# Cross-attention, one core: inputs transposed on the host, high parts converted by DMAs from GpSimd's queue

## The chip, the cores and the metric

The kernel runs on one NeuronCore of a Trainium2 chip. The metric is the device time of one execution in microseconds; the times shown are of three executions.

## The reference

`x` is (64, 256, 512), `ctx` is (64, 256, 384), all float32; the weights are (512, 512), (384, 512) and (512, 512).

```
Q = layer_norm(x @ W_text + b_text) * g1 + beta1
V = ctx @ W_audio + b_audio
K = layer_norm(V) * g2 + beta2
alpha = softmax(Q @ K.T / sqrt(512))          # per batch, 256 x 256
y = layer_norm((alpha @ V) @ W_out + b_out + x) * g_out + beta_out
```

## The kernel before, in words

The 64 batches are worked in N = 32 steps of two batches (512 tokens, T = 4 tiles of 128 rows). Every float32 matmul is made of three fp32r matmuls: each operand is split into a rounded high part and the rest, the low part, and hi\*hi + lo\*hi + hi\*lo are summed in PSUM (`product`, L253 to L255). Means are folded into the weights at the start; `W_audio` and `W_out` are multiplied together once (`wao`).

A step i does this, with j = i - 1, whose second half is worked off between:

- TensorE transposes ctx (`turn_c`, 3 groups of 4 transposes, for step i + 1) and x (`turn_x`, 4 groups) into the PSUM banks `turn`; ScalarE casts each bank to the high part (`cT_high`, `xT_high`), VectorE subtracts that from the bank to get the low part (`cT_low`, `xT_low`, the helper `low`, L613).
- `project_k`, `project_q` multiply them by the weights; ScalarE centres and squares. The sum of squares is made of `pair_squares` on GpSimd (L866), `add_square` (L637) and `sum_squares` (L645) on VectorE, `turn_sum` on TensorE and `sum_rows` on VectorE; GpSimd makes the reciprocal root (`row_rstd`, L872 and L874), and TensorE spreads it (`spread_rs`). VectorE scales (`k_norm`, `q_norm`) and makes low parts.
- `scores`, the softmax, and one step later `turn_p`, `probs_context` (context rows `c_hi`, `c_lo`, which GpSimd splits in `split_c`) and `output`.
- The residual: GpSimd adds the bias row to x into `y_rows[odd]` (`bias_x`, L895). VectorE adds the product (`y_sum`) and takes statistics, GpSimd makes scales (`y_scale`, L857 to L861), ScalarE normalises, GpSimd finishes (`finish_y`, L901, L903), SP stores (`store_y`).

There are two buffers `y_rows`, for even and odd steps. `y_rows[odd]` of step i is that of step i - 2, whose tiles 2 and 3 are finished and stored within step i.

There is no scheduler. Each engine has its queue in the order in which its block of the program is written, and waits on semaphores. The two orders that matter here:

- GpSimd's step: pair the squares of k, `finish_y(i-2)` for tiles 2 and 3, `row_rstd` of k, `bias_x` 0 and 1, pair the squares of q, `bias_x` 2 and 3, `row_rstd` of q, `split_c`, then the scales and `finish_y` of j for tiles 0 and 1. The first `bias_x` waits for all four tiles of x.
- SP's step: store tiles 2 and 3 of i - 2, copy `c_in` to `c_kept`, load `c_in` for i + 1, load the four tiles `x_in` for i + 1 (each when `bias_x` of step i has read it), store tiles 0 and 1 of i - 1.

`run_steps` writes steps 0, 1, N-2 and N-1 out and loops over pairs of the others.

Of the kernel before, what the change touches and what calls it, by code (L numbers as in the profile page):

```python
# [10 lines left out]
ALU = mybir.AluOpType  # L11
# [3 lines left out]
P = 128  # L15
# [3 lines left out]
def cross_attention_kernel(nc, x, ctx, w_text, b_text, w_audio, b_audio, w_out, b_out,  # L19
                           g1, beta1, g2, beta2, g_out, beta_out, out):  # L20

    B, L, D = x.shape
    S, DC = ctx.shape[1], ctx.shape[2]
    H = w_text.shape[1]
    NB = 2
    N = B // NB
    DT, CT, HT = D // P, DC // P, H // P  # L40
    LT, ST = L // P, S // P
    T = NB * LT
# [3 lines left out]
    x_v = x.rearrange("(i b) (t p) d -> i p (b t) d", b=NB, p=P)  # L46
    c_v = ctx.rearrange("(i b) (t p) d -> i p (b t) d", b=NB, p=P)
    out_v = out.rearrange("(i b) (t p) d -> i p (b t) d", b=NB, p=P)

    with ExitStack() as stack:  # L50
# [27 lines left out]
        x_in, c_in = sb("x_in", [P, T, D]), sb("c_in", [P, T, DC])  # L78
# [38 lines left out]
        x_loaded, c_loaded, c_copied = sem("x_loaded"), sem("c_loaded"), sem("c_copied")  # L117
# [15 lines left out]
        xT_done, cT_done = sem("xT_done"), sem("cT_done")  # L133
# [4 lines left out]
        xT_hi_made, cT_hi_made = sem("xT_hi_made"), sem("cT_hi_made")  # L138
# [49 lines left out]
        def _(sp):  # L188
            def load_c(i):
                sp.dma_start(c_in[:], c_v[i]).then_inc(c_loaded, 16)  # L190

            def load_x(i, t):
                sp.dma_start(x_in[:, t, :], x_v[i, :, t, :]).then_inc(x_loaded, 16)

            sp.dma_start(wa_stage[:, 0:CT, :], w_audio.rearrange("(t p) h -> p t h", p=P)).then_inc(wa_loaded, 16)
            load_c(0)
# [7 lines left out]
            for t in range(T):  # L204
                load_x(0, t)
# [4 lines left out]
            def store_y(j, odd, t):  # L210
                wait_apart(sp, y_ready, T * j + t + 1)
                sp.dma_start(out_v[j, :, t, :], y_rows[odd][:, t, :]).then_inc(stored[t], 16)

            def step(i, odd, first=False, last=False):
# [5 lines left out]
                wait_apart(sp, c_loaded, 16 * (i + 1))  # L220
                sp.dma_start(c_kept[:], c_in[:]).then_inc(c_copied, 16)
                if not last:
                    wait_apart(sp, c_copied, 16 * (i + 1))
                    wait_apart(sp, cT_done, CT * (i + 1))
                    load_c(i + 1)
                    wait_apart(sp, xT_done, DT * (i + 1))
                    for t in range(T):
                        wait_apart(sp, x_biased, T * i + t + 1)
                        load_x(i + 1, t)
# [15 lines left out]
        def _(pe):  # L245
# [32 lines left out]

            def turn_x(i, d):
                if d == 0:  # L280
                    pe.wait_ge(x_loaded, 16 * T * (i + 1))
                transposes(turn[d % 2], [x_in[:, t, d * P:(d + 1) * P] for t in range(T)]).then_inc(xT_done, 1)

            def turn_c(i, d):
                to = score[1] if d == 2 and isinstance(i, int) and i == 0 else turn[d % 2]
                if d == 0:
                    pe.wait_ge(c_loaded, 16 * (i + 1))
                transposes(to, [c_in[:, t, d * P:(d + 1) * P] for t in range(T)]).then_inc(cT_done, 1)
# [79 lines left out]
            for d in range(CT):  # L368
                turn_c(0, d)
# [5 lines left out]
            def step(i, odd, first=False, last=False):  # L375
# [53 lines left out]
                if not last:  # L429
                    pe.wait_ge(k_normed, HT * (i + 1))  # L430
                    turn_c(i + 1, 0)
                    pe.wait_ge(q_normed, HT * (i + 1))
                    turn_c(i + 1, 1)
                pe.wait_ge(kT_split, HT * (i + 1))
                scores(i, 0, 0)
                if not last:
                    pe.wait_ge(cT_split, CT * (i + 1) + 1)
                    turn_c(i + 1, 2)
# [22 lines left out]
        def _(act):  # L461
            def xT_high(i, d):
                act.wait_ge(xT_done, DT * i + d + 1)
                wait(act, q_done, T * i)
                nc.scalar.copy(xT_hi[:, d, :], turn[d % 2][:]).then_inc(xT_hi_made, 1)

            def cT_high(i, d):
                act.wait_ge(cT_done, CT * i + d + 1)
                wait(act, k_done, T * i)
                of = score[1] if d == 2 and isinstance(i, int) and i == 0 else turn[d % 2]  # L470
                nc.scalar.copy(cT_hi[:, d, :], of[:]).then_inc(cT_hi_made, 1)

# [70 lines left out]
            for d in range(CT):  # L543
                cT_high(0, d)
# [439 lines left out]
```

## Time and profile before

| | |
|---|---|
| time, median of 3 | 1487.2 us (1487.1, 1487.2, 1487.49) |
| span of the profiled execution | 1486.0 us |
| TensorE busy, share of the span | 1436.8 us, 97% |
| VectorE | 1147.9 us, 77% |
| GpSimd | 1050.5 us, 71% |
| ScalarE | 855.9 us, 58% |
| TensorE's granted clock, mean | 0.998 of full speed |
| HBM read, written | 62.40 MB, 33.55 MB |

The span reaches from the first to the last instruction. A time of the profiled execution itself is not listed beside its span; the three executions' times lie 1.1 to 1.5 us above it. Busy is the time in which at least one instruction of the engine runs; matmuls overlap each other, so their mean duration is longer than their pitch.

### The profile page before, as it was taken

Reading aid. Unit: us, or ns where it says so; the run is one execution under the profiler, and the core shown is the slowest. Engines: PE = TensorE matmul, PEld = TensorE weight load, DVE = VectorE, ACT = ScalarE, POOL = GpSimd, SP = SyncE. Lnnn points to the kernel's source line nnn. Section 1 sums busy time; section 2 is a strip of 40 time slices with the busy share of each in tenths; the row PEclk is TensorE's granted clock in tenths of the full one; section 3 lists DMA queues with packets and bytes.
Section 4 is the critical chain, followed back from the end, with each engine's and each line's share of the span. In section 5 each row is a group of like instructions: output and inputs, shape, how many; then the busy total and the mean of one; then the engine's idle time right before and its main releaser. Section 6 shows DMA issues by size and latency. Waiting matters only on the chain.

```text
span 1486.0 us, 26150 instructions
## 1 busy us (share of the span) xinstructions
PE 1436.8 (97%) x8240; PEld 1219.4 (82%) x8240; DVE 1147.9 (77%) x1657; ACT 855.9 (58%) x1547; POOL 1050.5 (71%) x1223
## 2 busy tenths in 40 slices
PE   8999999999999999999999999999999999999996
PEld 6788888888888888888888888888888888888885
DVE  6578777887777887777887778877778877788777
ACT  5465666555665555665556656556655466655563
POOL 2466777667867667776678676677776777766786
PEclk9999999999999999999999999999999999999999
DMA  5212221122221122211222211222212222112211
GB/s 191 71 43 86 100 99 53 67 85 92 99 99 46 66 90 93 99 67 53 85 92 99 99 49 64 92 92 99 84 43 78 92 99 99 51 67 87 93 50 58
DMA packets 63449, 121.44 MB, mean 82 GB/s; under 512 B 8385, under 2 KB 24769, under 8 KB 63425
## 3 DMA queue, kind: packets, MB, share of 16 engines
q1 hardware_dynamic: 63424, 121.14, 22.6%
q8 instruction: 12, 0.20, 0.1%
q14 instruction: 13, 0.10, 0.0%
HBM read 62.40 MB, written 33.55 MB: 65 GB/s over the span
## 4 chain that ended last, share of the span: by engine, by line
PE 33%; DVE 28%; POOL 23%; issue 12%; ACT 2%; DVEq 1%; SPq 1%; POOLq 0%; DMA 0%; ACTq 0%
POOL y_rows L901 8%; DVE qT_lo L663 8%; POOL y_rows L903 5%; DVE y_rows L685 5%; PE wide L255 5%; PE wide L253 5%; PE wide L254 5%; DVE q_cols L657 4%; PE turn L260 4%; DVE y_bn L690 3%; DVE row_max L700 3%; POOL squares L866 2%; DVE cT_lo L613 2%; POOL y_sc L859 2%; PE score L253 2%
## 5 line engine op out<-in xcount | busy, mean ns | idle before, releaser
L253 PE MATMUL wide<-xT_hi,wt_hi 128*128 128x512 f32 x512 | 209.9, 410 | 0.0
L255 PE MATMUL wide<-xT_hi,wt_lo 128*128 128x512 f32 x512 | 202.0, 395 | 0.0
L254 PE MATMUL wide<-xT_lo,wt_hi 128*128 128x512 f32 x512 | 201.9, 394 | 0.0
L895 POOL TENSOR_TENSOR y_rows<-x_in,bao_row 128x512 f32<-128x512 f32 x128 | 176.6, 1401 | 9.5 <-DVE bao_row L738 9.5
L507 ACT ACTIVATE qT_hi<-q_cols,beta_col 128x512 fp32r<-128x512 f32 x128 | 90.6, 725 | 154.7 <-DVE q_cols L657 154.7
L903 POOL TENSOR_TENSOR y_rows<-y_rows,betao_row 128x512 f32<-128x512 f32 x124 | 170.2, 1372 | 9.7
L901 POOL TENSOR_TENSOR y_rows<-y_rows,go_row 128x512 f32<-128x512 f32 x124 | 173.8, 1402 | 0.0
L657 DVE SCALAR_TENSOR_TENSOR k_cols<-k_cols,g_col,turn 128x512 f32<-128x512 f32 x128 | 89.6, 740 | 100.3 <-PE turn L260 100.3
L487 ACT ACTIVATE squares<-wide,btc_col 128x512 f32<-128x512 f32 x128 | 88.2, 689 | 135.4 <-PE wide L255 134.1
L857 POOL TENSOR_SCALAR y_sc<-y_mv 128x1 f32<-128x1 f32 x128 | 24.4, 191 | 192.6 <-DVE y_mv L695 187.2
L253 PE MATMUL wide<-cT_hi,wa_hi 128*128 128x512 f32 x384 | 159.3, 415 | 0.0
L335 PE MATMUL wide<-wao_hi,pcT_hi 128*128 128x512 f32 x384 | 154.2, 402 | 0.0
L255 PE MATMUL wide<-cT_hi,wa_lo 128*128 128x512 f32 x384 | 151.8, 395 | 0.0
L337 PE MATMUL wide<-wao_hi,pcT_lo 128*128 128x512 f32 x384 | 151.8, 395 | 0.0
L336 PE MATMUL wide<-wao_lo,pcT_hi 128*128 128x512 f32 x384 | 151.7, 395 | 0.0
L253 PE MATMUL score<-kT_hi,qT_hi 128*128 128x256 f32 x512 | 150.0, 293 | 1.4 <-DVE qT_lo L663 1.4
L254 PE MATMUL wide<-cT_lo,wa_hi 128*128 128x512 f32 x384 | 151.1, 393 | 0.0
L255 PE MATMUL score<-kT_hi,qT_lo 128*128 128x256 f32 x512 | 144.6, 282 | 0.0
L254 PE MATMUL score<-kT_lo,qT_hi 128*128 128x256 f32 x512 | 144.6, 282 | 0.0
L512 ACT ACTIVATE y_rows<-y_rows,y_sc 128x512 f32<-128x512 f32 x128 | 106.0, 828 | 62.7 <-POOL y_sc L861 62.7
L663 DVE SCALAR_TENSOR_TENSOR qT_lo<-q_cols,beta_col,qT_hi 128x512 fp32r<-128x512 f32 x128 | 138.0, 1096 | 4.4
L887 POOL TENSOR_TENSOR c_lo<-c_kept,c_hi 128x384 fp32r<-128x384 f32 x128 | 129.9, 1015 | 10.7
(116 smaller groups left out, 4081.1 us busy)
## 6 DMA issues: line engine op xcount, KB each, us to landing
x_in<-in_x SPq DMA_DIRECT2D x128, 256.0 KB, 4.3
out<-y_rows SPq DMA_DIRECT2D x128, 256.0 KB, 2.0
c_in<-in_ctx SPq DMA_DIRECT2D x32, 768.0 KB, 4.6
c_kept<-c_in SPq DMA_DIRECT2D x32, 768.0 KB, 3.5
q_cols<-in_L_xattn_W_text SPq DMA_DIRECT2D x1, 1024.0 KB, 5.6
y_rows<-in_L_xattn_W_out SPq DMA_DIRECT2D x1, 1024.0 KB, 8.1
k_cols<-in_L_xattn_W_audio SPq DMA_DIRECT2D x1, 768.0 KB, 4.7
bao_row<-in_L_xattn_b_out SPq DMA_DIRECT2D x1, 256.0 KB, 8.3
```

The lines of the kernel that those rows point to most:

```text
L253: nc.tensor.matmul(to, a_hi, b_hi, start=(m == 0), stop=False)
L254: nc.tensor.matmul(to, a_hi, b_lo, start=False, stop=False)
L255: done = nc.tensor.matmul(to, a_lo, b_hi, start=False, stop=(m == n - 1))
L335: nc.tensor.matmul(wide[t][:], hi, wao_hi[:, d, :], start=(d == 0), stop=False)
L336: nc.tensor.matmul(wide[t][:], hi, wao_lo[:, d, :], start=False, stop=False)
L337: done = nc.tensor.matmul(wide[t][:], lo, wao_hi[:, d, :], start=False, stop=(d == CT - 1))
L657: nc.vector.scalar_tensor_tensor(out=cols[:, h, :], in0=cols[:, h, :], scalar=gain[:, h:h + 1], in1=rs[:], op0=ALU.mult, op1=ALU.mult).the ...
L663: nc.vector.scalar_tensor_tensor(out=lo[:, h, :], in0=cols[:, h, :], scalar=shift[:, h:h + 1], in1=hi[:, h, :].bitcast(F32), op0=ALU.add, ...
L887: nc.gpsimd.tensor_tensor(c_lo[:, t, :], c_kept[:, t, :], c_hi[:, t, :].bitcast(F32), ALU.subtract).then_inc(c_split, 1)
L895: nc.gpsimd.tensor_tensor(y_rows[odd][:, t, :], x_in[:, t, :], bao_row[:], ALU.add).then_inc(x_biased, 1)
L901: nc.gpsimd.tensor_tensor(rows, rows, go_row[:], ALU.mult).then_inc(y_scaled, 1)
L903: nc.gpsimd.tensor_tensor(rows, rows, betao_row[:], ALU.add).then_inc(y_ready, 1)
```

## The change

The host lays out four arrays in place of two: `x_rows` and `c_rows` (per step, partition and tile, so that a partition's data is contiguous) and `xT` and `cT` (the transposes that TensorE made before). The output is written in the layout of `x_rows` and put back on the host.

- TensorE: `turn_x` and `turn_c` are gone.
- ScalarE: `xT_high` and `cT_high` are gone. GpSimd issues one DMA for each that reads `xT[i]` or `cT[i]` from HBM and converts it to fp32r on its way to `xT_hi` or `cT_hi`.
- VectorE: `xT_low` and `cT_low` subtract that from `xT_in` and `cT_in`, which SP loads from the same arrays; both inputs are in SBUF now.
- The rows of x are loaded by SP straight into `y_rows[odd]`, and `bias_x` adds the bias in place. The rows of ctx are loaded straight into `c_kept`. The tiles `x_in` and `c_in` are gone.

```diff
             def step(i, odd, first=False, last=False):
...
-                wait_apart(sp, c_loaded, 16 * (i + 1))
-                sp.dma_start(c_kept[:], c_in[:]).then_inc(c_copied, 16)
+                load_c(i)
                 if not last:
-                    wait_apart(sp, c_copied, 16 * (i + 1))
-                    wait_apart(sp, cT_done, CT * (i + 1))
-                    load_c(i + 1)
-                    wait_apart(sp, xT_done, DT * (i + 1))
-                    for t in range(T):
-                        wait_apart(sp, x_biased, T * i + t + 1)
-                        load_x(i + 1, t)
+                    wait_apart(sp, cT_split, CT * (i + 1))
+                    load_cT(i + 1)
...
+                for t in range(T):
+                    if not isinstance(i, int) or i >= 2:
+                        wait_apart(sp, stored[t], 16 * (i - 1))
+                    load_x(i, odd, t)
+                if not first and not last:
+                    wait_apart(sp, xT_split, DT * (i + 1))
+                    load_xT(i + 1)
...
             def xT_low(i, d):
-                dve.wait_ge(xT_hi_made, DT * i + d + 1)
-                low(xT_lo[:, d, :], turn[d % 2][:], xT_hi[:, d, :]).then_inc(xT_split, 1)
+                dve.wait_ge(xT_loaded, 16 * (i + 1))
+                dve.wait_ge(xT_hi_loaded, 16 * (i + 1))
+                low(xT_lo[:, d, :], xT_in[:, d, :], xT_hi[:, d, :]).then_inc(xT_split, 1)
...
+            def load_xT_high(i):
+                if not isinstance(i, int) or i > 0:
+                    wait_apart(pool, q_done, T * i)
+                nc.gpsimd.dma_start(xT_hi[:], xT[i]).then_inc(xT_hi_loaded, 16)
+
+            def load_cT_high(i):
+                if not isinstance(i, int) or i > 0:
+                    wait_apart(pool, k_done, T * i)
+                nc.gpsimd.dma_start(cT_hi[:], cT[i]).then_inc(cT_hi_loaded, 16)
...
                 if t == 0:
                     pool.wait_ge(x_loaded, 16 * T * (i + 1))
-                wait(pool, stored[t], 16 * (i - 1))
-                nc.gpsimd.tensor_tensor(y_rows[odd][:, t, :], x_in[:, t, :], bao_row[:], ALU.add).then_inc(x_biased, 1)
+                rows = y_rows[odd][:, t, :]
+                nc.gpsimd.tensor_tensor(rows, rows, bao_row[:], ALU.add).then_inc(x_biased, 1)
...
                 row_rstd(i, k_ssq_made, k_ssq, k_ve, k_rs, k_var, k_rstd)
+                if not last:
+                    load_cT_high(i + 1)
...
+                if not last:
+                    load_xT_high(i + 1)
                 for t in range(T):
                     split_c(i, t)
```

SP's queue before, a step of the loop, from the store of tile 3 of step i - 2 (`out` is the store; the bracket says which semaphore is waited for):

```order
L212 DMA out<-y_rows 128x512
L171 REGISTER_ALU
L171 ISA [waits c_split]
L221 DMA c_kept<-c_in 128x1536 [waits c_loaded]
L171 REGISTER_ALU [waits c_copied]
L190 ISA [waits cT_done]
L190 DMA c_in<-in_ctx 128x4x384
L171 REGISTER_ALU
L171 REGISTER_ALU [waits xT_done]
L193 ISA [waits x_biased]
L193 DMA x_in<-in_x 128x512
L171 REGISTER_ALU
```

and SP's queue in the changed kernel from the same store. The rows of x, which were for the next step, are now for this one and wait for the stores of step i - 2; a load of `cT_in` stands in front of them:

```order
L198 DMA out<-y_rows 128x512
L152 REGISTER_ALU
L177 ISA [waits c_split]
L177 DMA c_kept<-in_c_rows 128x1536
L152 ISA
L171 ISA [waits cT_split]
L171 DMA cT_in<-in_cT 128x1536
L152 ISA
L180 ISA [waits stored0]
L180 DMA y_rows<-in_x_rows 128x512
L180 ISA [waits stored1]
L180 DMA y_rows<-in_x_rows 128x512
```

The same pair of rows follows for tiles 2 and 3. The copy of c became a load, and the loads of x wait on `stored` in place of `x_biased`.

GpSimd's queue before, from the last `finish_y` of step i - 2:

```order
L903 TENSOR_TENSOR y_rows<-y_rows,betao_row 128x512 [waits y_scaled]
L171 REGISTER_ALU
L872 TENSOR_SCALAR k_ve<-k_ssq 128x4 [waits k_ssq_made]
L874 TENSOR_TENSOR k_rs<-k_ve,neg_half 128x4 [waits k_var]
L893 REGISTER_ALU
L165 ISA [waits x_loaded]
L895 TENSOR_TENSOR y_rows<-x_in,bao_row 128x512 [waits stored0]
L895 TENSOR_TENSOR y_rows<-x_in,bao_row 128x512 [waits stored1]
L866 TENSOR_TENSOR squares<-squares 128x512 [waits q_squared]
L895 TENSOR_TENSOR y_rows<-x_in,bao_row 128x512 [waits stored2]
L895 TENSOR_TENSOR y_rows<-x_in,bao_row 128x512 [waits stored3]
L872 TENSOR_SCALAR q_ve<-q_ssq 128x4 [waits q_ssq_made]
```

and in the changed kernel:

```order
L858 TENSOR_TENSOR y_rows<-y_rows,betao_row 128x512 [waits y_scaled]
L152 REGISTER_ALU
L827 TENSOR_SCALAR k_ve<-k_ssq 128x4 [waits k_ssq_made]
L829 TENSOR_TENSOR k_rs<-k_ve,neg_half 128x4 [waits k_var]
L152 REGISTER_ALU
L817 ISA [waits k_done]
L817 DMA cT_hi<-in_cT 128x1536
L848 REGISTER_ALU
L850 TENSOR_TENSOR y_rows<-y_rows,bao_row 128x512 [waits x_loaded]
L850 TENSOR_TENSOR y_rows<-y_rows,bao_row 128x512
L821 TENSOR_TENSOR squares<-squares 128x512 [waits q_squared]
L850 TENSOR_TENSOR y_rows<-y_rows,bao_row 128x512 x2
```

A DMA for `cT_hi` has come in behind k_rs; one for `xT_hi` comes behind q_rs, a few rows further on; the wait for x stands where it stood, and the waits for `stored` moved to SP's queue.

## Rows read from the trace of the kernel before

**Rows 1.** The page: engines' busy time, and the chain that ended last, by engine.

```profile
PE 1436.8 (97%) x8240; PEld 1219.4 (82%) x8240; DVE 1147.9 (77%) x1657; ACT 855.9 (58%) x1547; POOL 1050.5 (71%) x1223
...
PE 33%; DVE 28%; POOL 23%; issue 12%; ACT 2%; DVEq 1%; SPq 1%; POOLq 0%; DMA 0%; ACTq 0%
```

**Rows 2.** Timeline of POOL (start us, length, line, what, idle before), one step.

```profile
685.84 0.19 POOL L857 TENSOR_SCALAR y_sc<-y_mv 128x1 f32<-128x1 f32 x1 [4.60 <-DVE y_mv L695]
...
725.45 1.02 POOL L887 TENSOR_TENSOR c_lo<-c_kept,c_hi 128x384 fp32r<-128x384 f32 x1
731.07 0.19 POOL L857 TENSOR_SCALAR y_sc<-y_mv 128x1 f32<-128x1 f32 x1 [4.60 <-DVE y_mv L695]
```

**Rows 3.** Windows, one step: length, busy us of each engine, clock, DMA share, GB/s.

```profile
700.00:745.20 45.20, 44.29 (x258) 37.74 (x257) 35.43 (x52) 26.48 (x49) 32.99 (x39) 1.00 0.22 81
```

**Rows 4.** Timeline of POOL, around the end of the finish of step i-2.

```profile
700.86 1.63 POOL L903 TENSOR_TENSOR y_rows<-y_rows,betao_row 128x512 f32<-128x512 f32 x1
...
704.26 1.29 POOL L903 TENSOR_TENSOR y_rows<-y_rows,betao_row 128x512 f32<-128x512 f32 x1
...
706.90 2.53 POOL L895 TENSOR_TENSOR y_rows<-x_in,bao_row 128x512 f32<-128x512 f32 x2
709.38 1.75 POOL L866 TENSOR_TENSOR squares<-squares 128x512 f32<-128x512 f32 x1
```

**Rows 5.** Timeline of DVE, from the pairing of q's squares.

```profile
712.87 1.78 DVE L637 TENSOR_TENSOR squares<-squares 128x512 f32<-128x512 f32 x1
...
715.24 0.68 DVE L645 TENSOR_TENSOR square_sum<-squares 128x512 f32<-128x512 f32 x1
...
720.63 0.75 DVE L657 SCALAR_TENSOR_TENSOR q_cols<-q_cols,g_col,turn 128x512 f32<-128x512 f32 x1 [1.23 <-PE turn L260]
```

**Rows 6.** Timeline of PE: a group of transposes, and the two spreads.

```profile
699.78 0.60 PE L260 MATMUL turn<-ident,x_in 128*128 128x128 f32 x4
700.13 0.48 PE L253 MATMUL wide<-xT_hi,wt_hi 128*128 128x512 f32 x1
700.45 0.39 PE L254 MATMUL wide<-xT_lo,wt_hi 128*128 128x512 f32 x1
700.68 0.39 PE L255 MATMUL wide<-xT_hi,wt_lo 128*128 128x512 f32 x1
...
706.98 0.65 PE L260 MATMUL turn<-ident,k_rs 128*128 128x128 f32 x4 [0.45 <-POOL k_rs L874]
...
720.00 0.60 PE L260 MATMUL turn<-ident,q_rs 128*128 128x128 f32 x4
```

**Rows 7.** Groups by line: turns of c (busy, mean ns, idle before).

```profile
L260 PE MATMUL turn<-ident,c_in 128*128 128x128 f32 x380 | 54.3, 280 | 14.2 <-DVE cT_lo L613 14.2
```

**Rows 8.** Lines L613 and L637: ns min/median/max, first and last start.

```profile
L613 DVE TENSOR_TENSOR xT_lo<-turn,xT_hi x128: 675/681/692, 17.5 to 1425.1; 128x512 fp32r<-128x512 f32 x128
...
L637 DVE TENSOR_TENSOR squares<-squares x64: 675/1291/1786, 23.4 to 1436.7; 128x512 f32<-128x512 f32 x64
```

**Rows 9.** Timeline of SP's queue, one step (start us, length of issue).

```profile
706.38 0.50 SPq L221 DMA_DIRECT2D c_kept<-c_in  x1
710.28 0.41 SPq L190 DMA_DIRECT2D c_in<-in_ctx  x1
711.17 3.51 SPq L193 DMA_DIRECT2D x_in<-in_x  x4
```

**Rows 10.** The page: DMA issues (KB each, us to landing).

```profile
out<-y_rows SPq DMA_DIRECT2D x128, 256.0 KB, 2.0
```

**Rows 11.** Tile x_in, 690 to 750 us: landing.

```profile
DMA to landing us min/median/max: 3.3/4.4/4.5
```

**Rows 12.** Windows of 1 us: DMA share and GB/s in the last two columns.

```profile
711.00:712.00 1.00, 1.00 (x6) 0.83 (x5) 1.00 (x2) 1.00 (x3) 1.00 (x2) 1.00 0.45 61
...
714.00:715.00 1.00, 1.00 (x11) 1.00 (x10) 1.00 (x2) 0.92 (x3) 0.10 (x1) 1.00 1.07 408
...
716.00:717.00 1.00, 1.00 (x10) 1.00 (x10) 1.00 (x2) 0.59 (x1) 0.00 (x0) 1.00 0.92 305
```

More of the change, by code:

```diff
@@ L76, in cross_attention_kernel @@
         g2_col, beta2_col = sb("g2_col", [P, HT]), sb("beta2_col", [P, HT])
-        x_in, c_in = sb("x_in", [P, T, D]), sb("c_in", [P, T, DC])
+        xT_in, cT_in = sb("xT_in", [P, DT, T * P]), sb("cT_in", [P, CT, T * P])
         c_kept = sb("c_kept", [P, T, DC])
@@ L188, in _, with load_cT, load_xT, load_x @@
         def _(sp):
+            def load_cT(i):
+                sp.dma_start(cT_in[:], cT[i]).then_inc(cT_loaded, 16)
+            def load_xT(i):
+                sp.dma_start(xT_in[:], xT[i]).then_inc(xT_loaded, 16)
             def load_c(i):
-                sp.dma_start(c_in[:], c_v[i]).then_inc(c_loaded, 16)
-            def load_x(i, t):
-                sp.dma_start(x_in[:, t, :], x_v[i, :, t, :]).then_inc(x_loaded, 16)
+                sp.dma_start(c_kept[:], c_rows[i]).then_inc(c_loaded, 16)
+            def load_x(i, odd, t):
+                sp.dma_start(y_rows[odd][:, t, :], x_rows[i, :, t, :]).then_inc(x_loaded, 16)
             sp.dma_start(wa_stage[:, 0:CT, :], w_audio.rearrange("(t p) h -> p t h", p=P)).then_inc(wa_loaded, 16)
-            load_c(0)
+            load_cT(0)
             columns = [(ba_col, b_audio), (bt_col, b_text), (g1_col, g1), (beta1_col, beta1),
@@ L211, in store_y @@
                 wait_apart(sp, y_ready, T * j + t + 1)
-                sp.dma_start(out_v[j, :, t, :], y_rows[odd][:, t, :]).then_inc(stored[t], 16)
+                sp.dma_start(out[j, :, t, :], y_rows[odd][:, t, :]).then_inc(stored[t], 16)
             def step(i, odd, first=False, last=False):
@@ L238, in _ @@
                 sp.wait_ge(last_ready[by], count)
-                sp.dma_start(out_v[N - 1, :, t, :], y_rows[1][:, t, :]).then_inc(stored[t], 16)
+                sp.dma_start(out[N - 1, :, t, :], y_rows[1][:, t, :]).then_inc(stored[t], 16)
             for t in range(T):
@@ L277, in project_q @@
                 product(wide[h][:], terms, xT_split if h == 0 else None, DT * i).then_inc(q_done, 1)
[L279 to L288, printed above, removed]
             def turn_sum(i, to, summed, turned):
@@ L396, in step @@
                 project_q(i, 0)
+                if not first:
+                    pe.wait_ge(pT_split, NB * j + 1)
                 turn_sum(i, turn[0], k_summed, k_sum_turned)
@@ L461, in _ @@
         def _(act):
[L462 to L471, printed above, removed]
             def pT_high(j, b):
@@ L542, in _ @@
             wa_high()
-            for d in range(CT):
-                cT_high(0, d)
             waT_copy(2)
@@ L615, in xT_low @@
             def xT_low(i, d):
-                dve.wait_ge(xT_hi_made, DT * i + d + 1)
-                low(xT_lo[:, d, :], turn[d % 2][:], xT_hi[:, d, :]).then_inc(xT_split, 1)
+                dve.wait_ge(xT_loaded, 16 * (i + 1))
+                dve.wait_ge(xT_hi_loaded, 16 * (i + 1))
+                low(xT_lo[:, d, :], xT_in[:, d, :], xT_hi[:, d, :]).then_inc(xT_split, 1)
             def cT_low(i, d):
-                dve.wait_ge(cT_hi_made, CT * i + d + 1)
-                of = score[1] if d == 2 and isinstance(i, int) and i == 0 else turn[d % 2]
-                low(cT_lo[:, d, :], of[:], cT_hi[:, d, :]).then_inc(cT_split, 1)
+                dve.wait_ge(cT_loaded, 16 * (i + 1))
+                dve.wait_ge(cT_hi_loaded, 16 * (i + 1))
+                low(cT_lo[:, d, :], cT_in[:, d, :], cT_hi[:, d, :]).then_inc(cT_split, 1)
             def pT_low(j, b):
```

82 lines of the change are left out of this document (35 added, 47 removed).

## The prediction, made before the change was run

> **What bounds the kernel now.** I read the page first. TensorE is busy 97% of the span and the others 58 to 77% [rows 1], which invites the reading that TensorE is the bound and that each transpose taken away is won. The chain of the last work says otherwise: TensorE has 33% of it, VectorE 28%, GpSimd 23% [rows 1]. So I went on to one step in the middle. All steady steps are alike: GpSimd's first small operation on y_sc starts at 685.84 and again at 731.07, 45.2 us apart [rows 2], and a stretch of 45.2 us shows TensorE busy 44.3, VectorE 35.4, ScalarE 26.5, GpSimd 33.0 at full granted clock, 2.4 GHz [rows 3].
>
> The loop that closes on itself is this. GpSimd ends the last finish_y of step i-2 at 704.26 + 1.29 = 705.55 (I call this moment A), makes k_rs, starts to bias x at 706.90, biases two tiles of x, pairs the squares of q until 711.1 [rows 4]. VectorE takes the paired squares at 712.87 and has square_sum at 715.92 [rows 5]. TensorE turns it, runs on, and spreads q_rs at 720.00 [rows 6]. VectorE starts q_norm at 720.63 [rows 5]. GpSimd's y_scale begins 10.44 us later, at 731.07, and from the same place of the step before (685.84) to A it takes 19.71 us [rows 2, 4]. 10.44 + 19.71 = 30.15 us of the 45.2 lie there. TensorE waits in it for k_rs, 0.45 us [rows 6], so it is filled nearly to the brim but does not close the loop alone.
>
> **What goes.** TensorE loses seven groups of four transposes a step. A group starts 0.35 us before the next matmul, whose own pitch is 0.32 instead of 0.23 [rows 6]: 0.44 us a group, 3.1 us a step; the wait before the third turn of c, 0.46 us a step (14.2 in the kernel), goes too [rows 7]. TensorE would then need 44.3 - 3.1 = 41.2 us. ScalarE loses seven casts; with 58% busy [rows 1] it was never the bound, and I count nothing for it. On SP the copy c_kept<-c_in goes.
>
> **What VectorE gets.** The seven subtractions stay, but both inputs lie now in SBUF, where before one was in PSUM. All 128 of xT_lo took 675 to 692 ns, whatever GpSimd did; the sum of squares, with two SBUF inputs, took 675 to 1786 ns [rows 8]. So the seven cost between 0 and 7 x 1.1 = 7.7 us of VectorE's time a step. Most start where VectorE has idle time; in the loop above they can hold GpSimd's two last finish_y pairs and VectorE's statistics. On GpSimd's side one such operation took 1.63 us and the next of its kind 1.29 [rows 4]. I take 0 for the sum, and 2 us a step as the upper end. The Trainium skill, SBUF — State Buffer, section "Who interferes with whom", says that a VectorE instruction with two SBUF inputs contends with a GpSimd instruction that reads SBUF and that the pair of ports is a lock; the two spreads agree with it. By that rule the sum would lie above my 0, toward the upper end.
>
> **What SP and GpSimd get, and here I see the end being set.** Before, x_in was loaded a step ahead (four issues at 711.17 to 714.68 for the next step), and bias_x found it there. Now the rows of x go straight into y_rows[odd], which hold the output of step i-2 until it is stored. SP's order is: store tiles 2 and 3 of step i-2, load c_kept, load cT_in, then the four tiles of x. The store of tile 3 waits for A; before, SP issued the next DMA behind it, the copy of c, at 706.38 [rows 9]. So nothing of this step's x is even issued before A. Behind it stand 786 KB of c, 786 KB of cT and 1,049 KB of x: 2.62 MB. (Tile 3 also waits for its own store, 2.0 us [rows 10], which passes under the issues in front of it.) GpSimd's first bias_x waits for all four tiles, and it stands in GpSimd's queue ahead of the pairing of q's squares.
>
> How late are they? The load of c_in issued at 710.28 shows its first bytes in the slice from 711, about 1.3 us on; then the DMA engines are full (share 1.05 to 1.07) at 395 to 408 GB/s; the last bytes come in the slice that ends at 717, while the last x tile, issued 0.35 us before 714.68, takes at least 3.3 us to land, until some 717.6: 0.6 us from last byte to semaphore [rows 9, 11, 12]. For the change: 706.4 + 1.3, then 2.62 MB at 400 GB/s = 6.6 us, then 0.6: landed at 714.9, 9.35 us after A. The converting DMA of cT_hi is issued by GpSimd just behind k_rs, at about 707, and its 0.79 MB fall in the same full stretch: 2.0 us more if they share it evenly, 0 if they come behind. I take 2.0, because the rows show no free share: **L = 11.3 us** from A to x landed. Ends: 9.3 and 13.5 (the cast moving at half the rate). What a DMA issue costs GpSimd no row shows; one by SP takes 0.41 to 0.50 us [rows 9]. The first of GpSimd's two is under the wait for x, the second stands before split_c, which ended at 726.5, 4.6 us before GpSimd's next work [rows 2]: nothing as long as it stays under that. The Trainium skill, DMA: Bandwidth & Descriptors, section "Issuing engines are not separate DMA queues", says that DMAs from any engine run on the same 16 DMA engines and interleave; by that rule the 2.0 us belong in the sum, as I have taken from the full rows.
>
> **The new loop**, from x landed (X): two bias_x and the pairing, 3 x 1.28 = 3.9 with gaps [rows 4]; add_square, k_low and sum_squares 3.05, from 712.87 to 715.92 [rows 5]; from there to q_norm 4.71, with TensorE's queue between unchanged [rows 5, 6]; then 10.44 and 19.71 to the next A. Sum 41.8, plus L = 53.1 us a step instead of 45.2. With L at its old 1.35 this sum would be 43.2; the missing 2.1 us are VectorE's, which came to the paired squares only at 712.87. So x may land up to 712.87 - 3.9 = 708.97, that is A + 3.4, for free; 7.9 us of L are dear. TensorE waits them out before the turn of square_sum and before k_rs.
>
> Steps 2 to 31 have a predecessor whose rows they wait for: 30 x 7.9 = 237 us. Steps 0 and 1 and the ends I leave as they are. Span 1486.0 + 237 = 1723; the three runs lie 1.1 to 1.5 us above the span and their median 1.2, so **1724 us**.
>
> **The rivals.**
> 1. *TensorE is the bound and is relieved* (the other side). If x landed before A + 3.4, nothing above would happen: 32 x (3.1 + 0.46) = 114 us less, 1373; if the loop through GpSimd and VectorE holds as it does now, only the 0.7 us by which TensorE was late for q_rs (ready 719.27, spread 720.00) go: about 1465. For it: 97% busy. Against: 2.62 MB cannot pass in 3.4 us at 400 GB/s, and the order of the queues is fixed. Chance 0.06, mostly the second.
> 2. *The cast is dear.* GpSimd spends over 4.6 us on making a DMA, or the cast runs far below the 400 GB/s of [rows 12] and holds x back. 4 us a step more: 1844. No row speaks for or against. 0.10.
> 3. *The cast moves out of x's way* (it starts after x has passed, or costs the others nothing): L = 9.3, 51.1 us a step, 1664. This is inside my forecast's range. 0.2 of the 0.82 that the forecast holds.
> 4. *Both meet*: what the wait costs and what TensorE saves cancel to within 0.2% (3 us, about what a measurement can tell from no change). Only L near 3.4 does that. 0.02.
>
> **How the numbers follow.** The likeliest is 1724. Low end: L = 9.3 and 0.7 us a step gained on TensorE, 1643, and 10 us for the first steps: 1633. High end: L = 13.5 (66 more) and half of the contention (30 x 1): 1820, which takes in a part of rival 2. So 1633 to 1820. Slower 0.92, faster 0.06, same 0.02.
>
> **What would show it.** GpSimd idle about 9 us before the first bias_x of each step, released by the DMA of x rows; TensorE idle about 10 us a step before the turns of square_sum and k_rs, its busy share down to some 78%; steps 53 us apart; xT_lo and cT_lo with durations between 0.68 and 1.8 us. I am wrong if SP's x loads land before GpSimd has k_rs, if the step stays at 45 us or below, or if TensorE's idle time ends on something else than square_sum and k_rs.

## The result, and the profile after

The changed kernel takes 1877.8 us (median of 4, 1876.31 to 1878.75) beside 1487.35 us for the kernel before (1487.1 to 1488.35): ratio 1.2622, 95% interval 1.2604 to 1.264. It is slower, as forecast, but by 390 us and not by 237; the time lies above the range of 1633 to 1820. The wait for x that was forecast is there. Two costs beside it, which the forecast had at nothing, are there too: VectorE's operations with both inputs in SBUF, and TensorE's lower clock.

The page of the changed kernel (same parts as [rows 1]): busy time, the chain that ended last, some groups of instructions (busy and mean ns of one | idle time before them, and its releaser), and DMAs (KB each, median us from issue to landing).

```profile
span 1874.6 us, 24019 instructions
...
PE 1469.5 (78%) x7344; PEld 1207.3 (64%) x7344; DVE 1272.7 (68%) x1657; ACT 739.1 (39%) x1323; POOL 1135.5 (61%) x1287
...
POOL 36%; DVE 16%; DMA 15%; PE 14%; issue 11%; SPq 5%; ACT 2%; POOLq 0%; DVEq 0%
...
L850 POOL TENSOR_TENSOR y_rows<-y_rows,bao_row 128x512 f32<-128x512 f32 x128 | 173.2, 1369 | 314.5 <-DMA y_rows<-in_x_rows 314.5
L246 PE MATMUL wide<-xT_hi,wt_hi 128*128 128x512 f32 x512 | 235.3, 460 | 108.3 <-DVE xT_lo L557 107.2
L582 DVE TENSOR_TENSOR squares<-squares 128x512 f32<-128x512 f32 x64 | 109.0, 1703 | 253.4 <-POOL squares L821 253.4
L253 PE MATMUL turn<-ident,square_sum 128*128 128x128 f32 x256 | 69.7, 426 | 256.8 <-DVE square_sum L590 255.8
...
L557 DVE TENSOR_TENSOR xT_lo<-xT_in,xT_hi 128x512 fp32r<-128x512 f32 x128 | 199.9, 1600 | 0.7 <-DMA xT_hi<-in_xT 0.7
L858 POOL TENSOR_TENSOR y_rows<-y_rows,betao_row 128x512 f32<-128x512 f32 x124 | 188.6, 1521 | 9.7
...
xT_in<-in_xT SPq DMA_DIRECT2D x32, 1024.0 KB, 10.4
y_rows<-in_x_rows SPq DMA_DIRECT2D x128, 256.0 KB, 8.5
...
cT_hi<-in_cT POOLq DMA_DIRECT2D x32, 768.0 KB, 8.5
```

GpSimd's bias_x (L850) now waits 314.5 us for the DMA of the rows of x; VectorE (L582) waits 253.4 us for GpSimd's pair, and TensorE (L253) 255.8 us for square_sum: in the main one wait, handed on. TensorE is at 78%, as the signs said. Two things were not forecast: TensorE waits another 107 us for xT_lo, which takes 1600 ns on average where all 128 took 675 to 692 [rows 8], and rows of x take 8.5 us to land where they took 3.3 to 4.5 [rows 11].

GpSimd in one step, which answers to [rows 2, 4] (start, us, engine, operation):

```profile
935.74 1.60 POOL L858 TENSOR_TENSOR y_rows<-y_rows,betao_row 128x512 f32<-128x512 f32 x1
938.30 0.19 POOL L827 TENSOR_SCALAR k_ve<-k_ssq 128x4 f32<-128x4 f32 x1 [0.97 <-DVE k_ssq L595]
938.58 1.02 POOL L829 TENSOR_TENSOR k_rs<-k_ve,neg_half 128x4 f32<-128x4 f32 x1
939.57 0.65 POOL L817 DMA_DIRECT2D cT_hi<-in_cT  x1
949.85 2.50 POOL L850 TENSOR_TENSOR y_rows<-y_rows,bao_row 128x512 f32<-128x512 f32 x2 [9.63 <-DMA y_rows<-in_x_rows]
952.32 1.25 POOL L821 TENSOR_TENSOR squares<-squares 128x512 f32<-128x512 f32 x1
953.54 2.92 POOL L850 TENSOR_TENSOR y_rows<-y_rows,bao_row 128x512 f32<-128x512 f32 x2
...
974.61 0.43 POOL L802 TENSOR_SCALAR y_sc<-y_mv 128x1 f32<-128x1 f32 x1 [6.14 <-DVE y_mv L640]
```

The moment A is 935.74 + 1.60 = 937.34, and x has landed at 949.85: L = 12.5 us, with 9.63 of idle time. (This step is one of the shorter: in 24 steps between 200 and 1600 us L is 12.4 to 13.9, in the median 12.9.) SP's queue in the same step, which answers to [rows 9]:

```profile
938.25 0.35 SPq L177 DMA_DIRECT2D c_kept<-in_c_rows  x1
938.94 0.35 SPq L171 DMA_DIRECT2D cT_in<-in_cT  x1
939.62 2.26 SPq L180 DMA_DIRECT2D y_rows<-in_x_rows  x4
942.23 0.33 SPq L174 DMA_DIRECT2D xT_in<-in_xT  x1
```

Nothing of x is issued before A, as read from SP's order, and c_kept and cT_in go first. VectorE in the stretch behind, which answers to [rows 5]:

```profile
953.60 1.74 DVE L582 TENSOR_TENSOR squares<-squares 128x512 f32<-128x512 f32 x1 [6.85 <-POOL squares L821]
955.26 1.75 DVE L608 SCALAR_TENSOR_TENSOR kT_lo<-k_cols,beta_col,kT_hi 128x512 fp32r<-128x512 f32 x1
956.93 0.68 DVE L590 TENSOR_TENSOR square_sum<-squares 128x512 f32<-128x512 f32 x1
...
964.09 1.41 DVE L602 SCALAR_TENSOR_TENSOR q_cols<-q_cols,g_col,turn 128x512 f32<-128x512 f32 x2 [1.40 <-PE turn L253]
```

Two operations with their inputs in SBUF take 1.75 us while GpSimd biases x; the next, behind it, takes 0.68. And TensorE, its turn of square_sum:

```profile
957.66 1.11 PE L253 MATMUL turn<-ident,square_sum 128*128 128x128 f32 x4 [6.87 <-DVE square_sum L590]
```

and 1-us windows around it (length, TensorE busy with its instructions, granted clock, DMA share, GB/s):

```profile
952.00:953.00 1.00, 0.00 (x0) 1.00 0.00 0
...
955.00:956.00 1.00, 0.00 (x0) 0.50 0.00 0
...
959.00:960.00 1.00, 1.00 (x6) 0.50 0.00 0
961.00:962.00 1.00, 1.00 (x5) 0.71 0.00 0
963.00:964.00 1.00, 1.00 (x8) 1.00 0.92 328
```

TensorE idles 6.87 us; the granted clock falls to 0.50 (the lower level, 1.2 GHz) meanwhile. TensorE is at work again from 957.66 on, and the clock is back at 1.00 (2.4 GHz) between 961 and 963.

**The step, segment by segment.** Forecast 53.1 us, measured 57.8:

| segment | forecast | measured | why |
|---|---|---|---|
| A to x landed | 11.3 | 12.5 | xT_in, issued behind x, shares with it |
| x landed to square_sum | 6.95 | 7.8 (949.85 to 957.61) | a k_low at 1.75 where it took 0.74; add_square took 1.78 before, too |
| square_sum to q_norm | 4.71 | 6.5 (957.61 to 964.09) | TensorE at the lower clock |
| q_norm to y_scale | 10.44 | 10.5 (964.09 to 974.61) | |
| y_scale to A | 19.71 | 20.55 | finish_y held up by xT_low |

That is 4.7 us a step more, 141 us in 30 steps: of the 154 us missing all but 13 have a place. The steps between 400 and 1400 us take 58.1 us on average, 0.3 more than this one, which is most of the 13.

### The profile page after: what moved, and what is told of

It is laid out like the page before. It is cut to its first block, busy times and chain, and to the rows that moved or that the text cites. A ratio compares the mean times of both kernels' runs of the same rounds, so it can differ in the third digit from the quotient of the medians.

```text
span 1874.6 us, 24019 instructions
## 1 busy us (share of the span) xinstructions
PE 1469.5 (78%) x7344; PEld 1207.3 (64%) x7344; DVE 1272.7 (68%) x1657; ACT 739.1 (39%) x1323; POOL 1135.5 (61%) x1287
## 4 chain that ended last, share of the span: by engine, by line
POOL 36%; DVE 16%; DMA 15%; PE 14%; issue 11%; SPq 5%; ACT 2%; POOLq 0%; DVEq 0%
DMA y_rows<-in_x_rows 14%; POOL y_rows L856 10%; POOL y_rows L858 9%; POOL squares L821 5%; POOL y_rows L850 4%; DVE qT_lo L608 4%; POOL y_sc L804 4%; DVE squares L582 3%; DVE q_cols L602 3%; PE turn L253 3%; POOL y_sc L802 3%; SPq L180 2%; DVE y_rows L630 2%; PE wide L317 2%; POOL y_sc L806 2%
## 5 line engine op out<-in xcount | busy, mean ns | idle before, releaser
L850 POOL TENSOR_TENSOR y_rows<-y_rows,bao_row 128x512 f32<-128x512 f32 x128 | 173.2, 1369 | 314.5 <-DMA y_rows<-in_x_rows 314.5
L246 PE MATMUL wide<-xT_hi,wt_hi 128*128 128x512 f32 x512 | 235.3, 460 | 108.3 <-DVE xT_lo L557 107.2
L582 DVE TENSOR_TENSOR squares<-squares 128x512 f32<-128x512 f32 x64 | 109.0, 1703 | 253.4 <-POOL squares L821 253.4
L253 PE MATMUL turn<-ident,square_sum 128*128 128x128 f32 x256 | 69.7, 426 | 256.8 <-DVE square_sum L590 255.8
L253 PEld LDWEIGHTS turn<-ident,square_sum 128*128 128x128 f32 x256 | 45.1, 213 | 285.4 <-DVE square_sum L590 282.6
L246 PEld LDWEIGHTS wide<-xT_hi,wt_hi 128*128 128x128 f32 x512 | 105.9, 207 | 166.0 <-DVE xT_lo L557 147.2
L557 DVE TENSOR_TENSOR xT_lo<-xT_in,xT_hi 128x512 fp32r<-128x512 f32 x128 | 199.9, 1600 | 0.7 <-DMA xT_hi<-in_xT 0.7
L858 POOL TENSOR_TENSOR y_rows<-y_rows,betao_row 128x512 f32<-128x512 f32 x124 | 188.6, 1521 | 9.7
L802 POOL TENSOR_SCALAR y_sc<-y_mv 128x1 f32<-128x1 f32 x128 | 47.1, 368 | 185.4 <-DVE y_mv L640 176.7
L436 ACT CAST pcT_hi<-turn 128x512 fp32r<-128x512 f32 x32 | 18.8, 586 | 347.6 <-PE turn L248 347.4
```

Source lines behind the costliest of these rows:

```text
L246: nc.tensor.matmul(to, a_hi, b_hi, start=(m == 0), stop=False)
L253: done = nc.tensor.transpose(to[:, m * P:(m + 1) * P], b, ident[:])
L557: return nc.vector.tensor_tensor(to, whole, hi.bitcast(F32), ALU.subtract)
L582: nc.vector.tensor_tensor(squares[:, 2, :], squares[:, 0, :], squares[:, 2, :], ALU.add).then_inc(added, 1)
L850: nc.gpsimd.tensor_tensor(rows, rows, bao_row[:], ALU.add).then_inc(x_biased, 1)
L858: nc.gpsimd.tensor_tensor(rows, rows, betao_row[:], ALU.add).then_inc(y_ready, 1)
```

## The experiments

Short diffs are against the changed kernel unless another is named. Ratios are to the kernel before, on the same chip; it took 1486.7 to 1489.8 us there.

### The wait for x

**Late bias_x** (four `bias_x` behind `row_rstd` of q, where nothing near waits for them):

```diff
-                if not first:
-                    bias_x(i, odd, 0)
-                    bias_x(i, odd, 1)
                 pair_squares(...)
-                if not first:
-                    bias_x(i, odd, 2)
-                    bias_x(i, odd, 3)
                 row_rstd(i, q_ssq_made, ...)
+                if not first:
+                    for t in range(T):
+                        bias_x(i, odd, t)
```

> The changed kernel with one thing moved: GpSimd's four bias_x stand behind row_rstd of q, so that nothing urgent is queued behind the wait for x. Theory (the wait for x in front of the pairing of q's squares is the loss): x lands about 12.5 us after A, which is when q_rs is made anyway, the wait disappears from the loop, the step goes from 57.8 back to 45 to 47 us, the time to 1480 to 1540. Rival (the loss lies in VectorE's slower subtractions and TensorE's half clock, which the wait only accompanies): at least half of the 390 us stay, 1680 or more.

Measured: 1632.56 us, ratio 1.098 (1.0949 to 1.1012). Two groups of its page show that the wait for x falls from 314.5 to 10.8 us, and that the wait for xT_lo stays:

```profile
L246 PE MATMUL wide<-xT_hi,wt_hi 128*128 128x512 f32 x512 | 238.5, 466 | 99.7 <-DVE xT_lo L557 98.2
...
L850 POOL TENSOR_TENSOR y_rows<-y_rows,bao_row 128x512 f32<-128x512 f32 x128 | 175.3, 1394 | 10.8 <-DMA y_rows<-in_x_rows 10.8
```

So the move takes away 245 us. That this is close to the 237 forecast for the late rows is in part luck: the move takes away the wait, the lower clock behind it (1.8 us a step), and the biases beside add_square and k_low; the forecast priced the wait alone. The result lies between theory and rival: 145 us are left with next to no wait for x, so there is a second cause. xT_lo still takes 1.57 us on average, and TensorE waits 98 us for it.

**The rows of x first on SP** (`load_x` ahead of `load_c` and `load_cT`):

> The changed kernel with SP's loads of the x rows issued ahead of the loads of c_kept and cT_in, from step 1 on. Theory (x is late by the bytes in front of it): 1.57 MB at 400 GB/s are 3.9 us less, so x lands 8 to 9 us after A instead of 12.5, the step is 53 to 54 us, the time 1740 to 1770. Rival (x is late by the store of tile 3 and the latency of the chain store, wait, load, not by bytes): less than 1.5 us a step, 1835 or more.

Measured: 1790.65 us, ratio 1.2044 (1.1972 to 1.2115), between the two. SP's first row, then the end of finish_y (A) and the first bias_x on GpSimd:

```profile
946.98 2.89 SPq L180 DMA_DIRECT2D y_rows<-in_x_rows  x4
```

```profile
944.48 1.60 POOL L863 TENSOR_TENSOR y_rows<-y_rows,betao_row 128x512 f32<-128x512 f32 x1
...
956.64 2.52 POOL L855 TENSOR_TENSOR y_rows<-y_rows,bao_row 128x512 f32<-128x512 f32 x2 [7.68 <-DMA y_rows<-in_x_rows]
```

x is issued 0.9 us after A (946.08) and still needs until A + 10.6. My model of the queue (first issued, first landed, at 400 GB/s) would have had 1.3 + 2.6 + 0.6 us for it. The 1-us windows from 948 to the landing at 956.64 sum to 2.6 MB. The rows of x are 1.05 MB of that and the cast at most 0.79, so at least 0.76 MB belong to loads issued behind x. The start is slow besides: the first three windows move 0.31 MB at DMA shares of 0.99, 0.72 and 0.62; why is open.

**The same with the biases between**, behind `pair_squares` of q and ahead of `row_rstd` of q, and the cast of ctx later:

> Three moves together: SP loads x first, both converting DMAs behind row_rstd of q, and bias_x behind the pairing of q's squares but ahead of row_rstd of q, where the late-bias run leaves GpSimd 8 us idle. Theory (the idle stretch from A + 6 to A + 14 takes the bias once x lands at A + 8 or so, and y_scale is then not held up): the step falls from 50.0 to 47 to 48.5 us, 1540 to 1590. Rival (x lands only at A + 10 and bias pushes q_rs): 1620 or more.

Measured: 1637.92 us, ratio 1.1003 (1.0941 to 1.1066): the rival in the time. With the cast out of the way x lands earlier than the rival had it, at A + 8.4 in the median (7.7 to 9.9 in 28 steps), but the biases then push q_rs. No better place than the late bias was found.

### The converting DMAs

**The cast of ctx behind q_rs** in place of behind k_rs (`load_cT_high(i + 1)` moved down in GpSimd's step):

> The changed kernel with the converting DMA of cT_hi issued behind row_rstd of q instead of ahead of bias_x. Theory (the cast's 0.79 MB share the DMA engines with the rows of x and delay them): 2.0 us less a step, 1818. Rival (the cast gets its bytes out of x's way, or it is xT_in's 1 MB that shares): under 0.7 us a step, 1857 or more.

Measured: 1835.91 us, ratio 1.2348 (1.2312 to 1.2384). It takes away 42 us, 1.4 us a step, where the forecast had 2.0 in the sum. x lands at A + 11.1 in the median where it was A + 12.9, so of the wait itself 1.8 us go.

**ScalarE's casts again**, from `xT_in` and `cT_in`, no converting DMA:

> The changed kernel with ScalarE's seven casts back, reading xT_in and cT_in, and no converting DMAs. Theory (the casts by DMA cost only their share of the transfer in front of x, 1.3 us a step as the run with the later cast showed, and ScalarE has room): 1820 to 1860. Rival (the converting DMAs are a cost of their own on GpSimd or the rings): 1780 or less; or ScalarE's casts come onto the path of k's squares: above 1880.

Measured: 1808.37 us, ratio 1.2148 (1.2113 to 1.2184): 70 us less, between theory and rival. x lands at A + 10.9 in the median, hardly earlier than with the later cast; where the other 28 us lie was not separated.

**The same on top of the late bias:**

> The late-bias kernel with ScalarE's casts from xT_in and cT_in in place of the converting DMAs. Theory (with x out of the loop the DMAs' share of the transfers does not matter, only 0.65 us of issue on GpSimd behind q_rs, where GpSimd is late for y_scale): 0 to 0.7 us a step, 1610 to 1633. Rival (the casts by DMA carry a real part of the remaining 145 us): 1580 or less; or ScalarE's casts delay the centring of k: 1650 or more.

Measured: 1634.7 us, ratio 1.0986 (1.0954 to 1.1018): no difference from the late bias alone. So where x is waited for, the converting DMAs cost mainly by sharing with its rows. Where it is not, 0.7 us a step are saved on GpSimd between q_ve and y_scale and 0.8 between y_scale and A (medians), and ScalarE's casts take them back: k_ve waits 2.64 us for k_ssq in place of 0.96.

### The half clock

26 matmuls whose result nobody reads, into `turn[1]`, ahead of the turn of q's square_sum (they fill most of the idle 6.87 us; from step 1 on):

> The changed kernel with 26 matmuls of 512 columns put on TensorE ahead of the turn of q's square_sum (steps 1 to 31); they write a bank that is overwritten right after and are of no use. At 0.233 us each they take 6.1 of the 6.9 us in which TensorE waits there. Theory (the half clock behind the wait costs some 1.8 us a step): granted clock back to full there, from square_sum to q_norm 4.7 us instead of 6.5, 1815 to 1830. Rival (that stretch is longer for another reason): unchanged, 1870 to 1880.

Measured: 1862.37 us, ratio 1.2526 (1.2477 to 1.2575), nearer to the rival. VectorE, square_sum and then q_norm:

```profile
950.01 0.68 DVE L594 TENSOR_TENSOR square_sum<-squares 128x512 f32<-128x512 f32 x1
...
955.41 1.41 DVE L606 SCALAR_TENSOR_TENSOR q_cols<-q_cols,g_col,turn 128x512 f32<-128x512 f32 x2 [1.22 <-PE turn L254]
```

The granted clock is 1.00 in the windows of this stretch, and the segment from square_sum (950.69) to q_norm is 4.72 us, the forecast's 4.71. That shows the cause of that segment's 1.8 us. Yet the time falls by only 0.5 us a step: x lands a little later (A + 13.0 in the median, 12.9 before; 13.1 in this step), and y_scale comes 11.15 us after q_norm (955.41 to 966.56) in place of 10.5. The latter is the contention again: q_norm now comes while GpSimd is still in split_c, and VectorE's four qT_lo behind it take 5.06 us together, where they took 4.42. A segment's excess is not what its removal brings.

### Where the second operand lies

**Half the columns** in each xT_low from step 1 on, on top of the late bias (the low parts of the other half stay as they are):

> The late-bias kernel in which the four xT_low subtract only the first 256 of 512 columns from step 1 on (the other half of the low part stays that of step 0). Theory (the subtractions with two SBUF inputs, 1.75 us each beside GpSimd against 0.68 before, are what is left of the loss: they delay the squares of k and TensorE's project_q, and hold up finish_y): 4 x 0.85 = 3.4 us of VectorE a step less, the step falls by 2 to 3.4 us, 1525 to 1570. Rival (they are hidden, the rest is the late bias): less than 0.5 us a step, 1615 or more.

Measured: 1594.93 us, ratio 1.0715 (1.0684 to 1.0746), 38 us less than the late bias alone. Its tile xT_lo (count; min/median/max ns; first and last start):

```profile
L557 DVE TENSOR_TENSOR xT_lo<-xT_in,xT_hi x128: 418/1480/1522, 20.2 to 1526.6; 128x256 fp32r<-128x256 f32 x124, 128x512 fp32r<-128x512 f32 x4
```

Half the columns take 0.42 us alone and 1.48 beside GpSimd, all of them 0.68 and 1.75: 1.06 and 1.07 us are added, at either width. GpSimd's operations grow from 1.29 us to 1.46 beside the half width and 1.72 beside the whole. The numbers fit engines that take turns, one operation each, the two together as long as VectorE's own time plus 1.07 us of GpSimd's; what makes up the 1.07 no run shows. It is why halving the operation brought 38 us and not the 63 to 108 expected.

**The subtractions for the next step early**, at the end of VectorE's step, on top of the late bias:

> The late-bias kernel with the four xT_low of step i + 1 moved on VectorE from behind pT_low of step i + 1 to the end of step i, where VectorE waits some 4 us for the probabilities and GpSimd has small y_scale work. Theory (of the 5.4 us a step that the late-bias kernel has over the kernel before with the same move, 1.8 lie in GpSimd's finish_y held up by the lows, 0.8 in k_ssq coming after A, 1.5 in TensorE's half clock after it waited for the lows): most of these three go, the step falls from 50.0 to 46 to 47.5 us, 1510 to 1560. Rival (the contention only moves to finish_y of tile 1 and delays the softmax): 1600 or more.

Measured: 1573.97 us, ratio 1.0578 (1.0547 to 1.0608), 59 us less than the late bias alone, between theory and rival; the median xT_lo falls to 751 ns, and TensorE's wait for it from 98 to 0.7 us.

**The same with ScalarE's casts, also early:**

> Transposes from the host, ScalarE's casts, late bias, and the casts and lows of x both a step early (behind cT_high and behind the last y_moment). Theory (the wait for x, the collision of the lows with finish_y and the half clock are all the change costs, and TensorE's 3.1 us a step are a saving once they are gone): like the run with early lows less GpSimd's issues, 1480 to 1540; below 1471, the kernel before with late bias, only if TensorE's saving reaches the loop. Rival: the DVE subtractions from SBUF stay a cost wherever they stand: above 1560.

Measured: 1544.65 us, ratio 1.0381 (1.0351 to 1.0411). It ends just above the range I expected. This is the best form of the change found, and still slower than the kernel before.

**The one thing alone, in the kernel before.** Late biases first, against the kernel before:

> The kernel before with the same move as the run with the late bias (four bias_x behind row_rstd of q), to see what the move itself costs. GpSimd then has 5.2 us of bias and some 7.5 of split_c between q_rs (13.7 us after A) and y_scale (25.5 after A), 1 us too much. Theory (the late bias is itself a cost of about 1 to 2 us a step, and the rest of what the late-bias run has over the kernel before is the change's): 1500 to 1550. Rival (the order of GpSimd makes the whole 145 us): 1600 or more.

Measured: 1470.92 us, ratio 0.9882 (0.9853 to 0.991): a miss, and a gain. The biases no longer stand in front of the pairing of q's squares, nor beside add_square, which takes 0.68 us there in place of 1.78. Timed again:

> The same kernel as the experiment on the kernel before with late bias_x, timed beside the context experiment on the same chip: 1466 to 1476 us, 1.2% under the kernel before. If it were within 0.2% of the kernel before, the gain seen was the chip's and not the order's.

Measured: 1472.62 us, ratio 0.9888 (0.9873 to 0.9904). Then one line on top (the low products of x are left out in value by it, as the low part becomes zero):

```diff
-                low(xT_lo[:, d, :], turn[d % 2][:], xT_hi[:, d, :])
+                low(xT_lo[:, d, :], xT_hi[:, d, :].bitcast(F32), xT_hi[:, d, :])
```

> The kernel before with its four bias_x in a row behind row_rstd of q (as in the experiment before of that name), and one edit more: xT_low reads xT_hi as both inputs, so both lie in SBUF and no load, cast or transpose changes. (The low part of x becomes zero, so the low products of x are left out in value; all instructions run.) Theory: the four subtractions hold each other up with GpSimd's finish_y of tiles 2 and 3 as in the changed kernel: xT_lo mean 1.5 to 1.8 us instead of 0.68, finish_y 1.7 instead of 1.29, the step longer by 2 to 3.3 us than its base's 44.6: 1535 to 1575 us. Rival: the long subtractions of the changed kernel come from its DMAs (the converting ones above all), not from where the inputs lie: xT_lo stays at 0.68 to 0.9 and the time within 0.5 us a step of its base, 1455 to 1487.

Measured: 1601.54 us, ratio 1.075 (1.0734 to 1.0767), 129 us more than its base. VectorE in its base, add_square and an xT_low, then the same stretch with that line:

```profile
737.77 0.72 DVE L637 TENSOR_TENSOR squares<-squares 128x512 f32<-128x512 f32 x1
738.82 0.69 DVE L613 TENSOR_TENSOR xT_lo<-turn,xT_hi 128x512 fp32r<-128x512 f32 x1 [0.32 <-ACT xT_hi L465]
```

```profile
699.38 1.77 DVE L613 TENSOR_TENSOR xT_lo<-xT_hi 128x512 fp32r<-128x512 f32 x1
701.08 1.77 DVE L637 TENSOR_TENSOR squares<-squares 128x512 f32<-128x512 f32 x1
702.78 1.75 DVE L613 TENSOR_TENSOR xT_lo<-xT_hi 128x512 fp32r<-128x512 f32 x1
```

and TensorE with that line, a matmul and a window:

```profile
704.58 0.50 PE L253 MATMUL wide<-xT_hi,wt_hi 128*128 128x512 f32 x1 [2.32 <-DVE xT_lo L613]
```

```profile
708.00:709.00 1.00, 1.00 (x4) 0.50 1.02 424
```

No load, cast or transpose differs, and the operations, back to back, take 1.75 us where they took 0.7; the sums of squares are drawn in, since GpSimd is now held up too and is still at finish_y when they come. TensorE waits 2.32 us for xT_lo and is at the lower clock from 707 to 710. The picture is close to that of the changed kernel in its k half (929 to 941 us there), with none of its DMAs: the cause is where the inputs lie. The size came out above my expectation.

### The half of the change that might pay

On top of the late biases in the kernel before, only ctx from the host, cast by ScalarE; x as before (one line of the edit):

```diff
-                low(cT_lo[:, d, :], of[:], cT_hi[:, d, :])
+                low(cT_lo[:, d, :], cT_in[:, d, :], cT_hi[:, d, :])
```

> The kernel before with the late bias_x, and of the change only its half for ctx without the converting DMA: rows and transpose of ctx from the host, cast by ScalarE from cT_in; x stays as before (loaded a step ahead, turned by TensorE, low parts from PSUM). Theory: what the change loses, it loses by late rows of x and by xT_low beside GpSimd; the half for ctx has neither (cT_low runs at 0.68 us while GpSimd is quiet), so TensorE keeps the saving of three groups of transposes: a step of 42.8 to 43.6 instead of 44.6, 1410 to 1445 us. Rival: the loop over GpSimd and VectorE closes the step, not TensorE, and the saving is worth nothing: 1460 us or more.

Measured: 1489.4 us, ratio 0.9999 (0.999 to 1.0009): the rival, and 17 us slower than its base. GpSimd in the base, then here:

```profile
723.26 1.02 POOL L887 TENSOR_TENSOR c_lo<-c_kept,c_hi 128x384 fp32r<-128x384 f32 x1
724.36 0.19 POOL L857 TENSOR_SCALAR y_sc<-y_mv 128x1 f32<-128x1 f32 x1
```

```profile
728.60 1.36 POOL L869 TENSOR_TENSOR c_lo<-c_kept,c_hi 128x384 fp32r<-128x384 f32 x1
...
730.52 1.33 POOL L869 TENSOR_TENSOR c_lo<-c_kept,c_hi 128x384 fp32r<-128x384 f32 x1
731.93 0.19 POOL L839 TENSOR_SCALAR y_sc<-y_mv 128x1 f32<-128x1 f32 x1
```

cT_lo (0.68 us, begun between 728.4 and 732.3) now meets split_c: two c_lo are 0.33 us longer (1.36 and 1.33, for 1.00 and 1.02 in the base), and y_scale stands right behind them with no idle time. The step is 45.19 us (q_ve at 716.92 and 762.11) and that of the base 44.64 (709.99 and 754.63): 0.55 us. Two c_lo cost 0.66 of it, so at most 0.1 us a step is gained elsewhere: twelve transposes a step fewer are worth next to nothing, because TensorE does not close the loop.

## Why the prediction was right and wrong

- **What bounds the kernel; rival 1.** Right. TensorE's 97% was not a bound that relief would cash in: the context experiment saves transposes with nothing late, and what it gains is at most 0.1 us a step, less than its longer c_lo cost.
- **"So nothing of this step's x is even issued before A"** and the free A + 3.4. Right in place and near in size: 7.9 us a step forecast, 245 us in all measured by moving the biases. Of this 17 us come from the order alone, by the same move in the kernel before, and some from the clock and the contention behind the wait, so the nearness of 237 is partly luck.
- **L = 11.3.** Measured 12.5 here and 12.9 in the median. I let only what is issued ahead of x, and the cast, share with it: 3.41 MB. The windows from 939 to the landing at 949.85 sum to 3.9 MB, so some 0.5 MB of xT_in, issued 0.3 us behind the last tile of x, passed as well (x first on SP: A + 10.6, not the 5.4 that its order in the queue would give).
- **The 2.0 us for the cast.** Taken from full DMA rows, measured 1.8 of the wait and 1.4 of the step (42 us). The Trainium skill, DMA: Bandwidth & Descriptors, section "Issuing engines are not separate DMA queues", held in direction. The issue costs GpSimd 0.65 us, so rival 2, with its 4.6 us, fell; that its 1844 lies nearer to the result than my 1724 is chance.
- **"I take 0 for the sum, and 2 us a step as the upper end."** This step failed, and by what its removal brings it is the larger error. I weighed the seven subtractions by the rows in which one input was in PSUM, and where they start by VectorE's idle time, not by what GpSimd does then. The four xT_low run beside finish_y of tiles 2 and 3 back to back, at 1.75 us each. The rule I had beside it, the Trainium skill, SBUF — State Buffer, section "Who interferes with whom", was right, and the trace agrees: 0.68 us with GpSimd idle, 1.75 beside its operations. In the changed kernel 0.84 us a step of it show (finish_y held up); the rest is hidden under the wait for x. (Another operation, a k_low that now stands beside the biases of x, lengthens the stretch to square_sum by 0.8; its inputs were in SBUF before, too.) With the wait gone xT_low from SBUF costs 4 us a step, twice my upper end, by that one edit in the kernel before (129 us): I had priced the operations' length, not the wait of TensorE for xT_lo, its clock behind that, nor the hold on GpSimd. The three cT_low, at 0.65 to 0.69 us, are free in the changed kernel, because GpSimd idles there for 6.14 us.
- **"TensorE's queue between unchanged", 4.71.** This step failed, too. The order was unchanged, the clock was not: 6.5 us. An idle of 6.9 us, which I had forecast myself, brought the lower clock and 1.8 us; held up, the clock gives 4.72.

How the 390 us divide depends on what is taken away first, since the contention lies partly under the wait. By the step as it runs: 237 forecast, then 50 from the contention (0.84 and 0.8 a step), 53 from the clock, 36 from L, 2 behind q_norm and 13 without a place in the step shown. By removal: 245 with the wait for x, 145 left. The kernel with the late biases and its counterpart, the kernel before with the same move, can be laid side by side by four marks of GpSimd's step: the starts of k_ve and q_ve (the first operation of row_rstd of k and of q) and of y_scale, and the moment A. The table has medians of some 20 steps, in us; its last column is the counterpart with xT_low from SBUF.

| stretch | before, late bias | changed, late bias | before, xT_low from SBUF |
|---|---|---|---|
| q_ve to y_scale | 14.3 | 15.7 | 14.3 |
| y_scale to A | 18.4 | 20.1 | 19.4 |
| A to k_ve | 0.1 | 1.0 | 2.2 |
| k_ve to q_ve | 11.8 | 13.4 | 12.7 |

The last three rows hold 4.1 to 4.2 us of the difference (finish_y held up, k_ssq late, TensorE slower behind its wait for xT_lo); the one-line edit makes 4.0 in the same rows. The first row holds 1.3. Of it 0.7 are GpSimd's issue of the xT_hi DMA: with ScalarE's casts, and no such DMA, the stretch is 15.0. The other 0.7 are split_c, which runs beside cT_low then and takes 8.2 us (840.64 to 848.84) in place of 7.5; the context experiment has the same, and a stretch of 15.0, too. So cT_low is free only as long as x is waited for. The one-line edit divides its 4.0 otherwise (k_ssq later, finish_y held up less), so it is not shown that the two sums had to be equal. No form of the whole change beat the kernel before; the kernel before with late biases did, by 1.1% to 1.2%.

## What to carry to other kernels

Before an operand is moved from PSUM to SBUF, look on the timeline at what GpSimd does in that stretch: here VectorE's operations with both inputs in SBUF took turns with it, and both paid (1.75 us for 0.68, and 1.72 for 1.29). Before an input is loaded straight into the buffer that held an output, read off when that buffer comes free: a load that was a step ahead becomes one that starts when the store is issued. And when a forecast puts TensorE to idle for several us, price its clock behind the idle time as well (here 1.8 us behind 6.9), but do not count on getting all of that back (0.5 us a step).

## What the runs showed of the hardware

- VectorE's 128x512 subtraction with both inputs in SBUF: 0.68 us with GpSimd idle, 1.75 beside its tensor_tensor; 128x256: 0.42 and 1.48. GpSimd's 1.29 becomes 1.72 and 1.46.
- TensorE's granted clock fell from 1.00 to 0.50 within a 6.87 us idle and was back between 961 and 963, work having begun at 957.66. It was at 0.50 as well behind a wait of 2.40 us for xT_lo (changed kernel, 935 to 941) and in the experiment on the kernel before, where waits of 2.32 and 0.72 us came just before it.
- Loads issued later on the same queue shared with earlier ones: with x issued first, at least 0.76 of the 2.6 MB moved before its rows landed (at A + 10.6) belonged to loads behind it. Without the cast beside them (the run with the biases between) they landed at A + 8.4 in place of A + 10.3, in the medians.
- Issuing a converting DMA took GpSimd 0.65 us; 0.54 where it stood right behind another.
